# A third projection bank, mixed rows in pairs, and new orders in the token stage of an AdaLN-attention-FFN kernel

## The chip, the cores and the metric

One core of a Trainium2 chip runs the whole program. The metric is the device time of one execution in microseconds (us).

## The reference, cut to what matters

64 sequences of 64 tokens with 512 features pass through a conditioned mixing of tokens, a sparse attention and a residual, and then through a conditioned linear layer and a gated FFN with 4-bit weights and a second residual.

```python
h = einsum('bct,bcd->bdt', x, cond_weights[itok])          # tokens of a sequence mixed by a 64x64 matrix
q, k, v = h @ Wq + bq, h @ Wk + bk, h @ Wv + bv            # 16 query heads, 8 key heads of 32; rotary on q and k
mask = top 25 of 64 keys of each head by sigmoid(h @ Wr + br)
x1 = x + softmax(where(mask, q k^T / sqrt(32), -inf)) v @ Wo + bo
y = x1 @ W^T + scalings[i] * (x1 @ A[i]^T) @ Bm[i]^T       # i = adapter of the sequence
out = x1 + (gelu(y @ Wg^T) * (y @ Wu^T)) @ Wd^T            # 512 -> 4096 -> 512, weights dequantised on the chip
```

## The kernel before, in words

The program has a **token stage** and an **FFN stage**, one after the other on TensorE. The FFN stage (line 869, `product`, and line 886, `down_chunk`) is not touched by the change.

The token stage runs 16 iterations (`NT`) over tiles of 256 tokens, four sequences, which lie as two halves (q = 0, 1) of 128 rows. fp32 values are split into a high and a low part, and a product is three matmuls (high x high, high x low, low x high), so each value that comes out of PSUM and goes into a product passes twice: ScalarE copies the high part out (`mixed`, `heads_high`, `rows_high`), then VectorE subtracts it from the bank to get the low part (`mixed`, `heads_low`, `rows_low`) and frees the bank. Iteration t interleaves three tiles' work: the **body** of tile t (values v0, v1; scores; softmax; attention; output projection o0, o1), the **tail** of tile t-1 (adapter ranks xa and the linear layer h0 to h3, which go to DRAM in a combined form), and the **head** of tile t+1 (mixed rows hs0 to hs3, routing logits z, projections k0, k1, q0 to q3).

PSUM has eight banks, and all are used: two `proj` banks, which all the projections above take in the order of the list `USES` (20 uses, `BANK` gives the bank, `ready` waits until the previous use of the same bank was evacuated, `evacuated` waits for this use); two times two banks of `scores`, which the transposed probabilities share; one bank `pv` for probabilities times values; and one bank `turn` for x1 transposed.

The order is written out by hand on every engine, and the engines meet only at semaphores. On **TensorE**, `iteration` issues: `value` 0 and 1; `score` 0; `adapter_ranks`; `score` 1; `hidden_first` (h0, h1); `turn_probs` 0 (transposes of the softmax of half 0); `mixing` of chunks 0 and 1; `attend` 0; `mixing` of chunks 2 and 3; `routing`; k0, k1; `turn_probs` 1; `hidden_rest` (h2, h3); `out_proj` 0; `attend` 1; q0 to q3; `turn_rows` 0 (x1 of half 0 transposed); `out_proj` 1; `turn_rows` 1. `score` 0 waits for `q_ready`, that is for the low parts of q, one half of which VectorE makes in `q_low`.

On **VectorE**: values; `softmax_shift` 0 (row maximum, line 1248, and subtraction, line 1250); four steps of `dequantise` (lines 1156 to 1166); `mask_ranks`; `softmax_sum` 0 (line 1255); `ranks_low`; `normalise` 0 (line 1262), which releases `turn_probs` 0; `softmax_shift` 1; `mixed` of two chunks; three more steps of `dequantise` (lines 1169, 1172, 1176); `mixed` of the other two; `softmax_sum` and `normalise` 1; the last step of `dequantise`; `heads_low` 0; `rope` 0 (line 1213 on); `hidden_low` 0; `add_residual` 0; `top_keys`; `heads_low` 1; `rope` 1; `hidden_low` 1; `rows_low` 0; `add_residual` 1 (line 1278); `rope` 2; `q_low` (line 1223); `rows_low` 1. Iterations 0 and 1 dequantise a second unit of FFN weights.

On **ScalarE** among others: `exp`, `probs_turned` (line 987), `mixed` (line 947), `k_place` (eight copies on line 973, the last four of which wait for GpSimd's `k_low`, line 610), the copies of q0 to q3 out of PSUM with their bias (line 959), `rows_high`. On **GpSimd** each iteration begins when the store of x1 has landed (`x1_stored`): two adds of the residual (line 640), then the split or the combination of a unit of FFN weights (`store_unit`, lines 560 to 570), then the gathers of mixing matrices, `spread` (the combinations of h), `scale_unit`, loads, `k_low`, `spread`, `q_low`. `store_unit` is longest for a unit with odd k from 3 on (three combinations and three splits), which falls into iterations 2, 4, 8, 10 and 14. **SyncE** issues the transfers: logits out and in, h out, key bias out and in, x1 out.

## Time and profile before

| | before |
|---|---|
| median of 3 runs | 2682.28 us (2680.29 to 2684.94) |
| the profiled execution, its own time | 2682.33 us |
| its span in the trace | 2680.8 us |
| TensorE matmul busy | 2572.0 us (96%) |
| VectorE busy | 1963.3 us (73%) |
| ScalarE busy | 882.0 us (33%) |
| GpSimd busy | 977.0 us (36%) |
| token stage, to the first matmul of line 869 | 0 to 755.26 us |
| FFN stage | 755.26 to 2680.8 us |

The profile is one execution. [...] The share of busy time of a whole run says little here, since the two stages have different limits: the stretches of single iterations do. I cut the token stage at the starts of `score` 0 (line 731): 47.56, 93.24, 137.54, 182.87, 225.31, 271.25, 315.00, 357.48, 399.90, 445.19, 488.14, 534.03, 577.04, 619.98, 662.38 and 708.26 us for iterations 0 to 15.

### The profile page before, as it was taken

The numbers are of one execution on the slowest core, as the hardware profiler recorded it, in microseconds if no ns is written. First come the engines' busy times: TensorE is split into PE (matmuls) and PEld (weight loads), VectorE is DVE, ScalarE is ACT, GpSimd is POOL, SyncE is SP. The second block draws the span as 40 slices with busy tenths as digits, with TensorE's granted clock in tenths as the row PEclk, the third lists the DMA queues.
The fourth block names the chain that finished last, engine by engine and source line by source line (L and its number), as shares of the span: only waits on it lengthen the run. The fifth ranks groups of instructions, "written<-read, shape, count | busy, mean of one in ns | idle before, by whom it ended". The sixth has DMA issues, their size and how long they took to land.

```text
span 2680.8 us, 38725 instructions
## 1 busy us (share of the span) xinstructions
PE 2572.0 (96%) x13824; PEld 2163.0 (81%) x13824; DVE 1963.3 (73%) x3084; ACT 882.0 (33%) x1530; POOL 977.0 (36%) x1189
## 2 busy tenths in 40 slices
PE   5899999899889999999999999999999999999999
PEld 4788788788778888888888888888888888888887
DVE  6887878787768888888888888889754545454544
ACT  4445454444432222222222222222222222222222
POOL 3554435443445555545554555455500000000000
PEclk8999999999999999999999999999999999999999
DMA  3232222322598888786678667866557444565472
GB/s 121 77 102 93 91 97 91 105 78 92 188 335 315 331 322 327 275 336 236 242 276 330 242 239 279 324 243 238 208 191 276 186 156 150 220 244 194 175 260 102
DMA packets 167377, 562.27 MB, mean 210 GB/s; under 512 B 21784, under 2 KB 81048, under 8 KB 134560
## 3 DMA queue, kind: packets, MB, share of 16 engines
q1 hardware_dynamic: 131872, 458.10, 47.2%
q0 software_dynamic: 35328, 101.82, 10.2%
q8 instruction: 110, 1.80, 0.3%
q14 instruction: 67, 0.55, 0.1%
HBM read 427.27 MB, written 132.51 MB: 209 GB/s over the span
## 4 chain that ended last, share of the span: by engine, by line
PE 88%; DVE 8%; issue 2%; ACT 1%; SPq 0%; POOL 0%; DMA 0%; DVEq 0%; POOLq 0%; ACTq 0%
PE down L886 26%; PE bank_a L869 26%; PE bank_b L869 13%; PE proj L696 12%; PE bank_c L869 6%; PE scores L736 1%; PE pv L761 1%; PE scores L745 1%; DVE probs L1262 1%; DVE hs L1196 1%; DVE row_sum L1255 1%; DVE rope_sin L1216 1%; DVE row_max L1248 1%; ACT probsT L987 1%; DVE rope_in L1215 1%
## 5 line engine op out<-in xcount | busy, mean ns | idle before, releaser
L886 PE MATMUL down<-d_slot,inter_parts 128*128 128x512 f32 x3072 | 737.4, 389 | 0.0
L886 PEld LDWEIGHTS down<-d_slot,inter_parts 128*128 128x128 f32 x3072 | 576.6, 188 | 119.7
L1095 ACT ACTIVATE copy_p<-bank_a 128x512 f32<-128x512 f32 x384 | 229.7, 598 | 745.9 <-PE bank_a L869 745.9
L1404 DVE TENSOR_TENSOR acc<-down,acc 128x512 f32<-128x512 f32 x512 | 349.4, 686 | 67.4 <-PE down L886 60.1
L869 PE MATMUL bank_a<-h_ahead,gu_slot 128*128 128x512 f32 x1536 | 390.1, 389 | 2.5 <-ACT copy_p L1095 2.0
L869 PE MATMUL bank_a<-h_once,gu_slot 128*128 128x512 f32 x1536 | 390.0, 389 | 1.4 <-ACT copy_p L1095 1.4
L869 PEld LDWEIGHTS bank_a<-h_ahead,gu_slot 128*128 128x128 f32 x1536 | 288.1, 188 | 63.3 <-ACT copy_p L1095 2.9
L869 PEld LDWEIGHTS bank_a<-h_once,gu_slot 128*128 128x128 f32 x1536 | 288.1, 188 | 62.0 <-ACT copy_p L1095 2.2
L577 POOL TENSOR_TENSOR lut_v<-lut_v,signed_scale 128x512 f32<-128x512 f32 x96 | 123.9, 1290 | 422.1 <-DVE lut_v L1185 421.4
L1389 DVE TENSOR_TENSOR up<-gate,up 128x512 f32<-128x512 f32 x256 | 212.6, 830 | 88.9 <-ACT gate L1105 75.3
L1112 ACT ACTIVATE inter_parts<-up 128x512 fp32r<-128x512 f32 x256 | 160.3, 630 | 261.9 <-PE down L886 169.6
L1393 DVE TENSOR_TENSOR inter_parts<-up,inter_parts 128x512 fp32r<-128x512 f32 x256 | 186.9, 731 | 51.7 <-ACT inter_parts L1112 47.2
L562 POOL TENSOR_TENSOR w_parts<-lut_v,w_parts 128x512 fp32r<-128x512 f32 (+1 forms) x160 | 211.6, 1322 | 13.1
L1377 DVE TENSOR_TENSOR up<-bank_b,copy_p 128x512 f32<-128x512 f32 x128 | 87.8, 686 | 162.4 <-ACT copy_p L1095 141.0
L1105 ACT ACTIVATE gate<-bank_a 128x512 f32<-128x512 f32 x128 | 76.7, 599 | 374.5 <-PE bank_a L869 374.5
L869 PE MATMUL bank_b<-h_once,gu_slot 128*128 128x512 f32 x768 | 195.0, 389 | 0.0
L869 PE MATMUL bank_b<-h_ahead,gu_slot 128*128 128x512 f32 x768 | 194.9, 389 | 0.0
L869 PE MATMUL bank_c<-h_ahead,gu_slot 128*128 128x512 f32 x768 | 194.9, 389 | 0.0
L1370 DVE TENSOR_TENSOR gate<-bank_c,copy_p 128x512 f32<-128x512 f32 x128 | 88.5, 691 | 117.5 <-PE bank_c L869 114.3
L869 PEld LDWEIGHTS bank_b<-h_once,gu_slot 128*128 128x128 f32 x768 | 144.1, 188 | 30.3 <-DVE up L1377 0.4
L869 PEld LDWEIGHTS bank_c<-h_ahead,gu_slot 128*128 128x128 f32 x768 | 144.2, 188 | 30.0
L869 PEld LDWEIGHTS bank_b<-h_ahead,gu_slot 128*128 128x128 f32 x768 | 144.1, 188 | 30.0
(123 smaller groups left out, 3542.3 us busy)
## 6 DMA issues: line engine op xcount, KB each, us to landing
gu_slot<-w_scratch SPq DMA_DIRECT2D x128, 1792.0 KB, 7.6
d_slot<-d_scratch SPq DMA_DIRECT2D x64, 1024.0 KB, 9.8
w_scratch<-w_parts POOLq DMA_DIRECT2D x96, 512.0 KB, 4.3
h_ahead<-h_scratch SPq DMA_DIRECT2D x36, 1024.0 KB, 12.5
h_scratch<-h_out SPq DMA_DIRECT2D x32, 896.0 KB, 5.0
h_once<-h_scratch SPq DMA_DIRECT2D x27, 1024.0 KB, 7.9
acc<-out SPq DMA_DIRECT2D x18, 1024.0 KB, 5.5
out<-acc SPq DMA_DIRECT2D x18, 1024.0 KB, 11.6
```

What stands on the lines that cost most here:

```text
L562: pool.tensor_tensor(parts[:, :, LO, :], src, parts[:, :, HI, :].bitcast(F32), ALU.subtract).then_inc(w_step, 1)
L577: pool.tensor_tensor(lut_v[:, row], lut_v[:, row], signed_scale[:].bitcast(F32), ALU.mult).then_inc(w_step, 1)
L696: ins = pe.matmul(out_ap, lhsT, rhs, start=(start and n == 0), stop=(stop and n == len(pairs) - 1))
L869: ins = pe.matmul(bank[:], gu_slot[n % 2][:, w, u, c * P:(c + 1) * P], mat(v, h)[:, c, part, :], start=(start and c == 0 and i == 0), stop ...
L886: ins = pe.matmul(bank[:], inter_parts[:, j, u, q, e * P:(e + 1) * P], d_slot[m % 2][:, j, part, :], start=(j == 0 and i == 0), stop=(j == ...
L1095: act.activation(copy[:], bank_a[n % 2][:], ACT.Copy).then_inc(copied, 1)
L1112: act.activation(inter_parts[:, j, HI, q], up[:, q], ACT.Copy).then_inc(inter_hi[q], 1)
L1370: dve.tensor_tensor(gate[:, FIRST_HALF], bank_c[:], copy_p1[:], ALU.add).then_inc(gate_added[FIRST_HALF], 1)
L1377: dve.tensor_tensor(up[:, SECOND_HALF], bank_b[:], copy_p5[:], ALU.add).then_inc(up_added[SECOND_HALF], 1)
L1389: dve.tensor_tensor(up[:, q], gate[:, q], up[:, q], ALU.mult).then_inc(inter_done[q], 1)
L1393: dve.tensor_tensor(inter_parts[:, n % 2, LO, q], up[:, q], inter_parts[:, n % 2, HI, q].bitcast(F32), ALU.subtract) \
L1404: dve.tensor_tensor(acc[:, q, e], down[turn % 4][:], acc[:, q, e], ALU.add).then_inc(acc_added, 1)
```

## The change

The bank of `turn` is given up: `turn` becomes a view of the `pv` bank, and the free bank becomes a third `proj` bank. `attend` and `turn_rows` get a wait for each other's evacuation. The mixed rows come in pairs that fill a bank (`hs01`, `hs23`), so ScalarE and VectorE evacuate 512 columns at once, and `mixing` is issued whole ahead of `attend` 0. On TensorE `turn_rows` 1 moves from the end of its iteration to behind the two values of the next, h2 comes right behind `attend` 0 (h3 stays behind `turn_probs` 1). ScalarE and VectorE follow: `rows_high` 1 and `rows_low` 1 open the next iteration, h2's copy moves up, two of the four early steps of `dequantise` move behind the mixed rows, `mask_ranks` comes ahead of the other two, and VectorE's end of an iteration becomes `rope` 1, `rope` 2, `add_residual` 1, `q_low`, `rows_low` 0, `hidden_low` 1. SyncE stores x1 ahead of the second part of h.

```diff
@@ -151,12 +151,12 @@
             h_out = sb("h_out", [P, NM, 2, P], F32R)
-            proj = [ps(f"proj{i}", [P, 512], F32) for i in range(2)]
+            proj = [ps(f"proj{i}", [P, 512], F32) for i in range(3)]
 ...
             pv = ps("pv", [P, 2, 2, 2, C], F32)
-            turn = ps("turn", [P, KC, P], F32)
+            turn = pv[:].rearrange("p g r b c -> p g (r b c)").rearrange("p g (s n) -> p (g s) n", n=P)
@@ -191,8 +191,8 @@
         x_ld = [sem("x_ld0"), sem("x_ld1")]
-        proj_full = [sem("proj_full0"), sem("proj_full1")]
-        proj_free = [sem("proj_free0"), sem("proj_free1")]
+        proj_full = [sem(f"proj_full{i}") for i in range(3)]
+        proj_free = [sem(f"proj_free{i}") for i in range(3)]
@@ -236,10 +236,11 @@
         BODY = ["v0", "v1", "o0", "o1"]
-        HEAD = ["hs0", "hs1", "hs2", "hs3", "z", "k0", "k1", "q0", "q1", "q2", "q3"]
-        USES = ["v0", "v1", "xa", "h0", "h1", "hs0", "hs1", "hs2", "hs3", "z", "k0", "k1", "h2", "h3", "o0",
+        HEAD = ["hs01", "hs23", "z", "k0", "k1", "q0", "q1", "q2", "q3"]
+        USES = ["v0", "v1", "xa", "h0", "h1", "hs01", "hs23", "h2", "z", "k0", "k1", "h3", "o0",
                 "q0", "q1", "q2", "q3", "o1"]
-        BANK = {name: n % 2 for n, name in enumerate(USES)}
+        BANK = {name: n % 3 for n, name in enumerate(USES)}
+        PAIRS = {"hs01": (0, 1), "hs23": (2, 3)}
@@ -399,13 +400,13 @@
                     bias(t + 1)
-                if t > 0:
-                    store_hidden(t - 1, 1)
 ...
                 sp.dma_start(x1_v[t], x1[:]).then_inc(x1_stored, 16)
+                if t > 0:
+                    store_hidden(t - 1, 1)
@@ -696,21 +697,22 @@
-            def mixing(it, t, tt, par, chunks):
+            def mixing(it, t, tt, par):
 ...
                 pe.wait_ge(mix_ready, t * 2 + 2)
-                for c in chunks:
-                    bank, done = ready(it, f"hs{c}")
-                    for q in range(NP):
-                        ins = pe.matmul(bank[:, q * P:(q + 1) * P], x_in[:, par, q, c * P:(c + 1) * P],
-                                        mix_tile[:, par, q].rearrange("p b c -> p (b c)"), start=True, stop=True)
+                for name, pair in PAIRS.items():
+                    bank, done = ready(it, name)
+                    for n, c in enumerate(pair):
+                        for q in range(NP):
+                            ins = pe.matmul(bank[:, n * TOK + q * P:n * TOK + (q + 1) * P], x_in[:, par, q, c * P:(c + 1) * P],
+                                            mix_tile[:, par, q].rearrange("p b c -> p (b c)"), start=True, stop=True)
 ...
                 bank, done = ready(it, "z")
-                evacuated(pe, it, "hs2")
-                evacuated(pe, it, "hs3")
+                for name in PAIRS:
+                    evacuated(pe, it, name)
@@ -749,6 +751,7 @@
                 pe.wait_ge(pv_used, t * NP + q + PRIMED)
+                pe.wait_ge(turn_used, t * NP + PRIMED)
@@ -764,6 +767,7 @@
                 evacuated(pe, it, f"o{q}")
+                pe.wait_ge(pv_used, (t + 1) * NP + PRIMED)
@@ -795,10 +799,9 @@
-            def hidden_rest(it):
-                for n in (2, 3):
-                    hidden_main(it, n)
-                    hidden_adapter(n)
+            def hidden_rest(it, n):
+                hidden_main(it, n)
+                hidden_adapter(n)
@@ -807,6 +810,8 @@
                 value(it, 1)
+                if do_tail:
+                    turn_rows(t - 1, t - 1, 1)
@@ -819,16 +824,17 @@
                 if do_head:
-                    mixing(it, t + 1, tt_next, 1 - par, (0, 1))
+                    mixing(it, t + 1, tt_next, 1 - par)
                 attend(it, t, 0)
+                if do_tail:
+                    hidden_rest(it, 2)
                 if do_head:
-                    mixing(it, t + 1, tt_next, 1 - par, (2, 3))
 ...
                 if do_tail:
-                    hidden_rest(it)
+                    hidden_rest(it, 3)
@@ -838,9 +844,8 @@
                 out_proj(it, t, 1)
-                turn_rows(it, t, 1)
-
-            mixing(AHEAD, 0, 0, 0, range(KC))
+
+            mixing(AHEAD, 0, 0, 0)
@@ -855,9 +860,11 @@
             iteration(NT - 1, 1, 0, do_head=False)
+            turn_rows(NT - 1, NT - 1, 1)
 ...
             hidden_first(BEHIND, NT - 1)
-            hidden_rest(BEHIND)
+            hidden_rest(BEHIND, 2)
+            hidden_rest(BEHIND, 3)
@@ -941,10 +948,10 @@
-            def mixed(it, chunks):
-                for c in chunks:
-                    bank = full_wait(act, it, f"hs{c}")
-                    act.activation(hs[:, HI, c, :], bank[:, 0:TOK], ACT.Copy).then_inc(hs_hi, 1)
+            def mixed(it):
+                for name, (c, _) in PAIRS.items():
+                    bank = full_wait(act, it, name)
+                    act.activation(hs[:, HI, c:c + 2, :].rearrange("p k n -> p (k n)"), bank[:], ACT.Copy).then_inc(hs_hi, 1)
@@ -1016,6 +1023,8 @@
                 it = t
+                if do_tail:
+                    rows_high(t - 1, 1)
@@ -1025,11 +1034,11 @@
                 if do_head:
-                    mixed(it, (0, 1))
+                    mixed(it)
                 exp(t, 1)
-                if do_head:
-                    mixed(it, (2, 3))
                 heads_high(t, 0)
+                if do_tail:
+                    hidden(it, t - 1, 2)
@@ -1037,7 +1046,6 @@
                     hidden_high(t - 1, 0)
-                    hidden(it, t - 1, 2)
@@ -1054,7 +1062,6 @@
                     q_high(t + 1, 1)
-                rows_high(t, 1)
@@ -1062,7 +1069,7 @@
             split(3)
-            mixed(AHEAD, range(KC))
+            mixed(AHEAD)
@@ -1084,6 +1091,7 @@
             iteration(NT - 1, 1, do_head=False)
+            rows_high(NT - 1, 1)
@@ -1189,12 +1197,11 @@
-            def mixed(t, chunks):
-                for c in chunks:
-                    name = f"hs{c}"
-                    dve.wait_ge(hs_hi, t * KC + c + 1)
-                    dve.tensor_tensor(hs[:, LO, c, :], proj[BANK[name]][:, 0:TOK], hs[:, HI, c, :].bitcast(F32), ALU.subtract) \
-                       .then_inc(proj_free[BANK[name]], 1)
+            def mixed(t):
+                for name, (c, _) in PAIRS.items():
+                    dve.wait_ge(hs_hi, t * 2 + c // 2 + 1)
+                    hi, lo = (hs[:, u, c:c + 2, :].rearrange("p k n -> p (k n)") for u in (HI, LO))
+                    dve.tensor_tensor(lo, proj[BANK[name]][:], hi.bitcast(F32), ALU.subtract).then_inc(proj_free[BANK[name]], 1)
@@ -1295,22 +1302,22 @@
                 first, second = UNITS[t][0], (UNITS[t] + [None])[1]
+                if do_tail:
+                    rows_low(t - 1, 1)
 ...
                 softmax_shift(t, 0)
-                dequantise(*first, 0, 4)
 ...
                     mask_ranks(it, t - 1)
+                dequantise(*first, 0, 2)
 ...
                 if do_head:
-                    mixed(t + 1, (0, 1))
-                dequantise(*first, 4, DQ - 1)
-                if do_head:
-                    mixed(t + 1, (2, 3))
+                    mixed(t + 1)
+                dequantise(*first, 2, DQ - 1)
@@ -1329,14 +1336,13 @@
                     rope(it, t + 1, 1)
+                    rope(it, t + 1, 2)
+                add_residual(it, t, 1)
+                if do_head:
+                    q_low(t + 1)
+                rows_low(t, 0)
 ...
                     hidden_low(t - 1, 1)
-                rows_low(t, 0)
-                add_residual(it, t, 1)
-                if do_head:
-                    rope(it, t + 1, 2)
-                    q_low(t + 1)
-                rows_low(t, 1)
@@ -1345,7 +1351,7 @@
                               ALU.is_equal, ALU.mult).then_inc(const_made, 1)
-            mixed(0, range(KC))
+            mixed(0)
@@ -1359,6 +1365,7 @@
             iteration(NT - 1, do_head=False)
+            rows_low(NT - 1, 1)
```

## Rows read from the trace of the kernel before

**Rows 1.** Windows (us; busy and count of PE, PEld, DVE, ACT, POOL; PEclk; DMA): single stretches.
```profile
47.56:93.24 45.68, 35.51 (x265) 30.28 (x265) 37.95 (x69) 18.37 (x33) 11.98 (x14) 0.88 0.11 37
93.24:137.54 44.30, 40.75 (x337) 36.35 (x337) 40.26 (x74) 21.58 (x40) 22.80 (x27) 0.96 0.31 104
...
708.26:755.26 47.00, 38.21 (x284) 33.28 (x285) 22.58 (x33) 11.94 (x20) 13.35 (x21) 0.89 0.81 305
755.26:2680.80 1925.54, 1916.63 (x8448) 1585.12 (x8448) 1390.29 (x2034) 529.31 (x899) 653.28 (x790) 1.00 0.68 250
```
**Rows 2.** Windows of iterations 3, 5, 6, 7, 9, 11, 12, 13: one, and all eight's sum.
```profile
315.00:357.48 42.48, 39.20 (x336) 34.83 (x337) 33.37 (x65) 21.45 (x40) 17.20 (x21) 1.00 0.29 90
...
sum 342.39, PE 315.05 PEld 279.03 DVE 269.48 ACT 171.69 POOL 129.59; mean PE 39.38 PEld 34.88 DVE 33.69 ACT 21.46 POOL 16.20
```
**Rows 3.** Windows of iterations 2, 4, 8, 10, 14: one of them, and all five's sum.
```profile
225.31:271.25 45.94, 40.76 (x336) 35.90 (x337) 35.38 (x65) 21.44 (x40) 25.53 (x31) 0.96 0.30 100
...
sum 228.33, PE 204.17 PEld 179.38 DVE 175.75 ACT 106.69 POOL 121.05; mean PE 40.83 PEld 35.88 DVE 35.15 ACT 21.34 POOL 24.21
```
**Rows 4.** TensorE's waits in 0 to 760: waiter, releaser, us, times, longest.
```profile
PE proj L696 <- DVE hs L1196: 20.7, 16, 1.9
PE scores L731 <- DVE q_parts L1223: 16.8, 15, 5.7
PE turn L769 <- DVE x L1278: 13.6, 16, 1.8
...
PE scores L745 <- DVE probs L1262: 11.3, 12, 4.3
...
PE pv L761 <- ACT probsT L987: 5.6, 15, 1.2
```
**Rows 5.** Timeline of TensorE in iteration 6: start, us, line, tile, idle before.
```profile
324.42 1.09 PE L745 MATMUL scores<-identity,probs 128*128 128x128 f32 x8
...
330.28 1.53 PE L696 MATMUL proj<-hs,wr 128*16 128x256 f32 x12 [1.02 <-DVE hs L1196]
...
353.18 0.66 PE L769 MATMUL turn<-identity,x 128*128 128x128 f32 x4 [0.79 <-DVE x L1278]
```
**Rows 6.** The same in iteration 4: the routing matmuls.
```profile
242.50 2.63 PE L696 MATMUL proj<-hs,wr 128*16 128x256 f32 x12 [1.94 <-DVE hs L1196]
```
**Rows 7.** Critical chain: routing, k0 and k1 of iterations 4 and 6.
```profile
242.50 5.96 PE proj L696 x36
...
330.28 4.41 PE proj L696 x36
```
**Rows 8.** Timeline of VectorE in iteration 6: rope 1, hidden_low 1, q_low.
```profile
346.99 0.01 DVE L1213 LOAD_MASK_SELECT rope_sin<-rope_in  x1 [0.31 <-ACT rope_in L959]
...
350.59 1.09 DVE L1291 TENSOR_TENSOR h_out<-h_mats,h_out 128x896 fp32r<-128x896 f32 x1 [0.77 <-ACT h_out L1015]
...
356.53 0.69 DVE L1223 TENSOR_TENSOR q_parts<-rope_in,q_parts 128x512 fp32r<-128x512 f32 x1 [0.70 <-ACT q_parts L978]
```
**Rows 9.** Single lines over 50 to 756: ns min/median/max (dequantise, normalise).
```profile
L1164 DVE TENSOR_SCALAR signed_scale<-packed x18: 279/332/1380, 54.3 to 713.3; 128x256 int32<-128x256 int32 x18
L1262 DVE TENSOR_TENSOR probs<-probs,row_inv x32: 1210/1224/2298, 56.6 to 723.4; 128x1024 f32<-128x1024 f32 x32
```
**Rows 10.** Timeline of GpSimd: residual adds of iteration 4, k_low of iteration 8.
```profile
226.23 2.54 POOL L640 TENSOR_TENSOR x<-x_in,bo 128x512 f32<-128x512 f32 x2 [5.50 <-DMA out<-x]
426.91 1.40 POOL L610 TENSOR_TENSOR rope_in<-rope_in,k_whole 128x512 f32<-128x512 f32 x1 [1.40 <-ACT k_whole L963]
```
**Rows 11.** Timeline of ScalarE in iteration 6: k_place, second half.
```profile
342.01 2.55 ACT L973 ACTIVATE k_diagonal<-rope_in 32x512 fp32r<-32x512 f32 x4
```
**Rows 12.** Timeline of TensorE in iteration 15: turn_probs 1 and out_proj 1.
```profile
724.72 1.97 PE L745 MATMUL scores<-identity,probs 128*128 128x128 f32 x8 [2.85 <-DVE probs L1262]
...
737.79 2.97 PE L696 MATMUL proj<-wo,attnT 128*128 128x512 f32 x12 [0.94 <-DVE attnT L1266]
```
**Rows 13.** The same at the start: mixed rows of tile 0, second pair.
```profile
16.10 2.08 PE L706 MATMUL proj<-mix_tile,x_in 128*128 128x128 f32 x8 [1.59 <-DVE hs L1196]
```

## The prediction, made before the changed kernel was built or run

> **What bounds the kernel now.** The page comes first: TensorE is busy 96% of the span, but this is a mean over two stages. The windows separate them. In the FFN stage TensorE is busy 1916.63 of 1925.54 us at full clock [rows 1]; the change touches none of it, and there is nothing left to gain there. The token stage is different. Its inner iterations come in two kinds. Eight of them, which I call light (42.80 us on average, 342.39 / 8), hold 39.38 us of TensorE work [rows 2]. Five, which I call heavy (45.67 us, 228.33 / 5), have the longest work on GpSimd, 24.21 us against 16.20, and a granted clock of 0.96 instead of 1.00 [rows 2, 3]. In both kinds VectorE is busy only 34 to 35 us and ScalarE 21, so TensorE is the bound, together with the points at which it stands still.
>
> TensorE's waits name these points [rows 4], and the timeline of iteration 6 shows them in place [rows 5]. Of its 42.48 us it is idle 3.28 (42.48 - 39.20) [rows 2]. Four waits make 2.9 of that: 1.02 before the routing for the low parts of the mixed rows, 0.79 before `turn_rows` 1 for x1 [rows 5], 0.8 before `score` 0 for `q_low` (16.8 us in 15, of which one is 5.7) and 0.3 in `attend` 0 for the transposed probabilities (5.6 in 15, longest 1.2) [rows 4]. The rest, 0.4, lies inside `attend` and stays. So the floor of an inner iteration without the four is 42.5 - 2.9 = 39.6 us. The light mean lies 0.3 above iteration 6 because `turn_probs` 0 sometimes waits for `normalise` 0: 11.3 us in 12 waits, of which 4.3 in iteration 0 and 2.85 in iteration 15 [rows 4, 12].
>
> A heavy iteration costs 2.87 more than a light one. The routing waits 1.94 instead of 1.02 [rows 5, 6], and the 36 matmuls behind this wait take 5.96 us instead of 4.41, at the lower of the two clocks for a part of it [rows 7]: 0.92 + 1.55. The remaining 0.4 is a longer wait at `turn_probs` 0.
>
> **The change part by part.**
>
> *Mixed rows whole and ahead of `attend` 0, h2 behind it.* No matmul is added or dropped. Between the last mixing matmul and the routing now lie `attend` 0 (1.4 us) and h2 (15 matmuls, at 4.41 / 36 = 0.12 us each 1.8 us) [rows 7]: 3.2 us of cover for one ScalarE copy and one VectorE subtraction of 512 columns, about 0.6 us each by the like ones. Since `attend` 0 starts one pair of mixing matmuls later (0.9 us), the 0.3 wait for the transposed probabilities goes as well. The wait of 1.02, and in heavy iterations that of 1.94, goes; next due there is h2's evacuation before k1 reuses its bank, some 2 us early. With it the slow clock behind this wait goes, 1.55 in a heavy iteration: the wait of 1.94 is followed by it, that of 1.02 is not [rows 5 to 7]. What h2 covers is taken from behind `turn_probs` 1, where TensorE has other work.
>
> *`turn_rows` 1 behind the two values.* Its wait of 0.79 is covered by 24 value matmuls, 2.9 us. But VectorE now runs `rope` 2 ahead of `add_residual` 1, and `turn_rows` 1 must also find `rows_low` 0 done, which stands behind `q_low`; `score` 0 is queued behind it on TensorE, and with it everything. I count from `turn_probs` 0 (324.42 = T) [rows 5]. TensorE: `turn_rows` 1 started at T+28.76; without its wait (0.79) and the two above it (1.02, 0.3), plus 2.9 for the values, it is wanted at T+29.6. VectorE: `rope` 1 started at T+22.57 [rows 8]. It hangs on the copy of q1, which hangs on q1's matmuls (1.3 earlier) and on the end of `k_place` (T+20.14, now 0.3 earlier) [rows 11]; I take T+21.4. `q_low` started at T+32.11 [rows 8]. It loses the 1.1 of the earlier start, the 1.8 of `hidden_low` 1 and its wait, `rows_low` 0 with the small wait behind it (0.8), and the 0.6 of `add_residual` 1, which now hides in the wait for `q_high`: T+27.8. One subtraction for `q_low` and one for `rows_low` 0 end at T+29.1. Cover left over: 0.5 us. If it isn't enough, the excess is paid one for one.
>
> *`q_low` earlier.* `score` 0 wants it at T+30.0, it is there at T+28.4: the wait of 0.8 goes. Moved behind it are `hidden_low` 1, `rows_low` 1 and the values' additions; they end some 2.3 us after `score` 0 begins, just when the first softmax can begin, so they cost nothing as long as `turn_rows` 1 is on time.
>
> *Two `dequantise` steps fewer ahead of `softmax_sum` 0, two more behind the mixed rows.* A step takes 0.28 us alone and up to 1.38 [rows 9]. Ahead of `normalise` 0 this is worth 0.6 to 2 us, which is what the waits at `turn_probs` 0 are made of; but `softmax_sum` 0 can't start before `exp`. Behind the mixed rows the steps lie ahead of `normalise` 1, where none of the 13 inner iterations shows a wait [rows 4]. I take 0.1 to 0.2 us left over in light iterations. `normalise` takes 1.21 us, or 2.30 when disturbed [rows 9], and that is the 0.9 that I leave in the heavy ones.
>
> The stretched rows point to GpSimd: they stand beside its long work. [...]
>
> *SyncE and GpSimd.* x1 is stored ahead of h's second part, so nothing is queued in front of it. But `add_residual` 1 now comes relatively later: it ended 4.35 us before the next `score` 0 and will end 2.4 before. GpSimd starts its iteration 5.5 us behind it [rows 10], hence 2.0 later against `score` 0. In light iterations there is slack. In heavy ones GpSimd's `k_low` had 1.40 us to spare in iteration 8 [rows 10], the head's chain gets 2.5 faster (0.92 + 1.55) and GpSimd 2.0 later, so `k_low` comes 3.1 late, of which about 1.1 hides behind the first half of `k_place` (2.55 against `k_low`'s 1.40) [rows 10, 11]. The 2.0 left over shift the copies of q and the tail of VectorE, less the cover of 0.5 and what the wait at `turn_probs` 0 gives back: I take 0.9 per heavy iteration, between 0 and 2.5.
>
> *Third bank.* In the new order q2 reuses o0's bank and q3 that of q0; with two banks q1 waited for o0 and q2 for q0, and TensorE, now earlier against ScalarE, would have waited there. It gains nothing alone. *Shared bank.* `attend` waits for `rows_low` 1, done ten us before; `turn_rows` 0 waits for `heads_low` 1, which `out_proj` 1 needs 0.4 us later anyway. Price 0, but in iteration 15, where no q projection lies between, about 0.4 of the wait of 0.94 [rows 12] is paid twice.
>
> **The sum**, against the profiled execution (2682.33 us; 1.5 around its span of 2680.8):
> - light: floor 39.6 + 0.2 = 39.8, saved 3.0 x 8 = 24.0 (bounds 39.5 to 40.6: 26.4 to 17.6)
> - heavy: 39.6 + 0.9 + 0.9, rounded up to 41.5, saved 4.16 x 5 = 20.8 (40.3 to 43.0: 26.8 to 13.3)
> - iterations 0 and 1: VectorE is busy 37.95 and 40.26 us [rows 1] and sets the pace; ahead of `score` 0 it drops 0.7 and 1.8 us of work, and iteration 0 fills the routing wait: 3.7 (1.5 to 6)
> - iteration 15: h2 fills 1.8 of the 2.85 wait, of which VectorE's two extra steps take 0.4 back; less 0.4 for the shared bank, plus 2.0 of the slow clock behind that wait (8 transposes 1.97 instead of 1.09 and the matmuls after them) [rows 5, 12]: 3.0 (0.5 to 5.5)
> - before iteration 0: the wait of 1.59 between the two mixed pairs goes [rows 13]; weights are still loading and being split, so I take 1.0 (0 to 1.6)
>
> Together 52.5 us, bounds 33 to 66. The profiled execution is at the median of the runs (2682.33 against 2682.28), so no correction is needed: 2682.3 - 52.5 = 2629.8 us.
>
> **The rivals.**
> - *GpSimd becomes the limit of heavy iterations.* For it: a spare of only 1.40, 2.0 lost. Against: the first half of `k_place`. They stay at 44.0: 5 x 2.5 = 12.5 us less gain, 2642.
> - *VectorE meets GpSimd in new places.* The adds and splits of GpSimd now stand beside `softmax_sum` and `normalise` 0 instead of the steps before them. If each iteration pays one stretched `normalise` (1.09) and part of a stretched step, 1.4 in all for 13 iterations, the time is 2630 + 18 = 2648.
> - *The tail binds, and the clock falls with it (slower).* The place is `turn_rows` 1 behind the values, with `score` 0 behind it. If VectorE's chain to `rows_low` 0 ends 2.9 later than I count (0.5 cover), TensorE waits 2.4 at one point, and as behind the waits of 1.94 the slow clock adds 1.55: 3.95 against 2.9 saved, 13 x 1.05 = 14 slower, 2696. It decides from 1.9 late on (a wait of 1.4 with slow clock gives back the 2.9). Against it: I find no 1.9 us in this chain, whose steps are all in the trace.
> - *The waits only move* and the time stays at 2682: TensorE's order is strict, so a wait removed at one place may be met at the next. Against it: the covers worked out above.
>
> **How the numbers follow.** Forecast 0.64, GpSimd's limit 0.12, the new meetings 0.16, no change 0.03, slower 0.05. Of these the first three are faster: 0.92. A measurement of this kernel can tell 0.2%, 5.4 us, from no change. The range takes the bounds of the sum, 2616 to 2649, and both milder rivals: 2615 to 2650.
>
> **What would show it.** TensorE's waits for line 1196's rows and for `q_parts` and x gone from inner iterations; light iterations 39.6 to 40.0 us between `score` 0; PEclk 1.00 in iterations 2, 4, 8, 10, 14; the FFN stage at 1925.5 us. A wait of `turn_rows` 1 or of `score` 0 behind it above 0.5 us would prove the tail's count wrong; a wait of k_diagonal's second half for `k_low` above 2 us the first rival; a `normalise` of 2.3 us in light iterations the second.

## The result, and the profile after

The changed kernel takes 2646.5 us (median of 4 runs, 2645.14 to 2652.3) where the kernel before took 2683.61 in the same comparison (4 runs). The ratio is 0.987 [0.9858, 0.9882]: 1.3% faster. The profiled execution has a span of 2646.0 us against 2680.8, so 34.8 us went. The forecast was 52.5 us and 2629.8; the time lies inside the range of 2615 to 2650, at its upper edge. So the direction was right and a third of the gain is missing, and the question is where it stayed.

As before, I cut the token stage at the starts of `score` 0 (now line 733). In the rows PE is TensorE (PEld its weight loads), DVE VectorE, ACT ScalarE, POOL GpSimd and SP SyncE; "xN" counts instructions; brackets give the idle time of an engine before a row and who ended it; PEclk is the granted TensorE clock as a share of the full one. First single windows of the changed kernel (us; busy and count of PE, PEld, DVE, ACT, POOL; PEclk; DMA): iterations 0, 1 and 15 and the FFN stage, which answer to [rows 1].

```profile
44.75:92.50 47.75, 38.47 (x265) 32.47 (x265) 38.09 (x66) 17.14 (x28) 11.98 (x14) 0.80 0.10 33
92.50:136.78 44.28, 39.26 (x337) 34.93 (x337) 40.76 (x70) 21.42 (x37) 22.17 (x27) 1.00 0.26 84
675.47:720.24 44.77, 36.50 (x285) 31.86 (x285) 23.18 (x34) 12.46 (x21) 13.59 (x21) 0.92 0.85 319
720.24:2646.00 1925.76, 1916.96 (x8448) 1585.53 (x8448) 1391.69 (x2034) 529.61 (x899) 654.05 (x790) 1.00 0.67 250
```

Then the light iterations, which answer to [rows 2]: 3, 6 and 12 of the eight, and the sum.

```profile
178.45:220.56 42.11, 40.18 (x337) 36.31 (x337) 34.62 (x63) 21.07 (x37) 16.86 (x21) 0.96 0.30 95
...
304.15:344.86 40.71, 38.78 (x337) 34.86 (x337) 34.95 (x63) 21.07 (x37) 17.12 (x21) 1.00 0.31 94
...
551.78:593.88 42.10, 40.18 (x338) 36.17 (x337) 34.13 (x63) 21.07 (x37) 14.79 (x19) 0.96 0.29 90
...
sum 329.92, PE 314.54 PEld 283.21 DVE 278.00 ACT 168.58 POOL 130.13; mean PE 39.32 PEld 35.40 DVE 34.75 ACT 21.07 POOL 16.27
```

And the heavy ones, which answer to [rows 3]: 4 and 8 of the five, and the sum.

```profile
220.56:263.42 42.86, 40.62 (x337) 36.34 (x337) 36.12 (x63) 20.96 (x37) 25.07 (x31) 0.96 0.32 108
385.60:427.29 41.69, 39.07 (x338) 34.92 (x337) 37.12 (x63) 21.07 (x37) 24.33 (x30) 1.00 0.34 111
...
sum 208.77, PE 196.62 PEld 176.00 DVE 183.91 ACT 105.25 POOL 120.06; mean PE 39.32 PEld 35.20 DVE 36.78 ACT 21.05 POOL 24.01
```

Set beside the terms of the sum, the windows give this:

| term | predicted | measured |
|---|---|---|
| 8 light iterations | 24.0 | 342.39 - 329.92 = 12.5 |
| 5 heavy iterations | 20.8 | 228.33 - 208.77 = 19.6 |
| iterations 0 and 1 | 3.7 | 89.98 - 92.03 = -2.05 |
| iteration 15 | 3.0 | 47.00 - 44.77 = 2.2 |
| before iteration 0 | 1.0 | 47.56 - 44.75 = 2.8 |
| FFN stage | 0 | 1925.54 - 1925.76 = -0.2 |
| sum | 52.5 | 34.8 |

So the light iterations miss 11.5 us and iterations 0 and 1 miss 5.7; the rest is right within 2 us. TensorE's waits of the token stage (waiter, releaser, us, times, longest) say what is new, if laid beside [rows 4]:

```profile
PE pv L773 <- DVE x1T L1279: 28.5, 16, 2.7
...
PE proj L697 <- ACT rope_in L966: 6.0, 4, 4.2
...
PE scores L733 <- DVE q_parts L1230: 5.2, 1, 5.2
...
PE scores L747 <- DVE probs L1269: 2.8, 2, 2.6
PE proj L697 <- DVE wq L1198: 1.9, 1, 1.9
PE proj L697 <- DVE hs L1204: 1.5, 1, 1.5
...
PE pv L764 <- ACT probsT L994: 1.2, 1, 1.2
```

Three of the forecast's four waits are gone from the inner iterations: the routing's for the mixed rows (20.7 us in 16, now 1.5 in 1), `score` 0's for `q_low` (16.8 in 15, now only the first, 5.2) and `attend` 0's for the transposed probabilities (5.6 in 15, now 1.2 in 1). Most of `turn_probs`' went too (11.3 in 12, now 2.8 in 2). In their place `turn_rows` (line 773) waits 28.5 us in 16 for VectorE's low part of the rows, where it had waited 13.6 us for x. This is the first item of the forecast's own list of what would prove it wrong ("a wait of `turn_rows` 1 or of `score` 0 behind it above 0.5 us would prove the tail's count wrong").

The timeline of the end of iteration 6 (start, us, line, tile, idle before and releaser) shows the chain behind that wait. VectorE:

```profile
335.01 0.01 DVE L1220 LOAD_MASK_SELECT rope_sin<-rope_in  x1 [0.29 <-ACT rope_in L966]
...
337.15 0.69 DVE L1225 TENSOR_TENSOR rope_in<-rope_in,rope_sin 128x512 f32<-128x512 f32 x1
338.21 0.01 DVE L1220 LOAD_MASK_SELECT rope_sin<-rope_in  x1 [0.38 <-DVE rope_in L1225]
...
339.03 0.69 DVE L1222 TENSOR_TENSOR rope_in<-rope_in,cos 128x512 f32<-128x512 f32 x1
339.63 1.80 DVE L1223 TENSOR_TENSOR rope_sin<-rope_sin,sin 128x512 f32<-128x512 f32 x1
341.47 0.69 DVE L1225 TENSOR_TENSOR rope_in<-rope_in,rope_sin 128x512 f32<-128x512 f32 x1
342.08 0.68 DVE L1285 TENSOR_TENSOR x<-proj,x 128x512 f32<-128x512 f32 x1
342.86 0.69 DVE L1230 TENSOR_TENSOR q_parts<-rope_in,q_parts 128x512 fp32r<-128x512 f32 x1
343.47 0.68 DVE L1279 TENSOR_TENSOR x1T<-pv,x1T 128x512 fp32r<-128x512 f32 x1
```

GpSimd and TensorE in the same stretch:

```profile
339.11 1.78 POOL L616 TENSOR_TENSOR q_parts<-rope_in,q_parts 128x512 fp32r<-128x512 f32 x1 [7.74 <-ACT q_parts L985]
...
344.30 0.63 PE L773 MATMUL pv<-identity,x 128*128 128x128 f32 x4 [1.57 <-DVE x1T L1279]
```

With T = 313.44, where `turn_probs` 0 starts, `rope` 1 begins at T+21.57; the forecast said T+21.4. But `rows_low` 0 ends at T+30.71 and not T+29.1. Two things lie between that the count did not have. `rope` 2 stands directly behind `rope` 1 and begins 0.38 us after its last sum. Inside a rope, where an operation also waits for the one ahead of it, the gap is 0.03 to 0.04 us, so the dependence alone is not the price; between two ropes the program has three waits and three semaphore increments on VectorE's queue, and no run shows which of them takes the time. And the product with the sine takes 1.80 us instead of 0.68, beside GpSimd's own `q_low`, which itself takes 1.78. Against a cover of 0.5 us, 0.38 + 1.1 was too much. TensorE, too, was ready earlier, at T+29.29 and not T+29.6; `turn_rows` 1 starts at T+30.86, which is the wait of 1.57.

In the kernel before the same GpSimd operation ran beside other work. First VectorE, then GpSimd:

```profile
351.60 0.68 DVE L1272 TENSOR_TENSOR x1T<-turn,x1T 128x512 fp32r<-128x512 f32 x1
352.44 0.69 DVE L1278 TENSOR_TENSOR x<-proj,x 128x512 f32<-128x512 f32 x1 [0.15 <-PE proj L696]
...
351.64 1.29 POOL L615 TENSOR_TENSOR q_parts<-rope_in,q_parts 128x512 fp32r<-128x512 f32 x1 [9.53 <-ACT q_parts L978]
```

There VectorE read one operand from PSUM (`turn`, `proj`) and one from SBUF, and all three took their ordinary time (0.68, 0.69 and GpSimd's 1.29 us). The products of `rope` read both operands from SBUF. So the traces show a difference by the kind of operand: 1.80 us with two SBUF inputs, 0.68 and 0.69 with one. They also give the size of the stretch. Wherever a product or sum of a rope is stretched (in the changed kernel 22 times from 60 us on), it ends 0.54 to 0.56 us after the end of the GpSimd operation that was running when it began: 341.43 against 339.11 + 1.78 = 340.89 here. These products and sums began 0.03 to 0.62 us into GpSimd's operation, so what sets their end is the end of GpSimd's operation and not how long ago it began.

In heavy iterations GpSimd's `q_low` falls onto the product with the cosine instead, which then takes 1.53 or 1.54 us (1.82 in iteration 14) and not 0.69.

### The profile page after: what moved, and what is told of

The parts are those of the page before. It is cut to its first block, busy times and chain, and to the rows that moved or that the text cites. A ratio compares the mean times of both kernels' runs of the same rounds, so it can differ in the third digit from the quotient of the medians.

```text
span 2646.0 us, 38647 instructions
## 1 busy us (share of the span) xinstructions
PE 2562.0 (97%) x13824; PEld 2162.5 (82%) x13824; DVE 1982.4 (75%) x3052; ACT 876.3 (33%) x1498; POOL 977.0 (37%) x1189
## 4 chain that ended last, share of the span: by engine, by line
PE 84%; DVE 8%; ACT 4%; issue 2%; DMA 1%; POOL 0%; DVEq 0%; SPq 0%; ACTq 0%; POOLq 0%
PE down L893 26%; PE bank_a L876 26%; PE bank_b L876 13%; PE proj L697 7%; PE bank_c L876 6%; ACT k_diagonal L980 2%; PE scores L738 2%; DVE rope_sin L1223 2%; DVE rope_in L1222 2%; DVE rope_sin L1220 1%; DVE rope_in L1225 1%; PE proj L708 1%; PE pv L764 1%; DMA h_scratch<-h_out 1%; ACT rope_in L966 1%
## 6 DMA issues: line engine op xcount, KB each, us to landing
h_ahead<-h_scratch SPq DMA_DIRECT2D x36, 1024.0 KB, 12.5
```

## The experiments

The theory after the result: *VectorE's chain from `rope` 1 to `rows_low` 0 sets the end of an inner iteration, and GpSimd's `q_low` stretches it.* The rivals: that TensorE's own order (the clock, the banks) or VectorE's new order is what costs, and that the other moved steps brought less than I took. Times below are medians of 4 runs (experiment 6: 10; the last two: 5). The kernel before took 2683.92 us beside the first four kernels, 2683.55 beside the next three and 2683.45 beside the last two, so all ratios have the same base; a difference from the changed kernel is one from 2646.5.

**1. A narrow `q_low` on GpSimd.** It makes the low part for one of its four sequences only and leaves it out for the other three.

```diff
-            def q_low(t):
+            def q_low(t, blocks=NB):
...
+                pool.tensor_tensor(q_parts[:, LO, 0].rearrange("p b r c -> p r b c")[:, :, 0:blocks],
...
-                    q_low(t + 1)
+                    q_low(t + 1, 1)
```

> The changed kernel, in which GpSimd's q_low of the iterations computes one of the four sequences' columns only (the low part of half of q is left out for the other three). Theory: in the changed kernel TensorE's wait of 1.57 us at turn_rows 1 comes from VectorE's second rope behind the first, where the product with sin takes 1.80 us instead of 0.69 because it meets GpSimd's q_low (1.77 us). Then the product takes 0.7 to 0.9 us, the wait falls to about 0.5 us, and the time by about 1.1 us in 13 iterations, 12 to 18 us, to 2628 to 2635 (ratio to before 0.980 to 0.982). Rival: the wait is the length of the chain alone (ropes one behind the other, subtractions); then the product stays at 1.8 or something else takes its place, and the time stays at 2646 (0.987).

Measured: 2629.89 us, ratio 0.9803 [0.9785, 0.9821], 16.6 us less. VectorE and GpSimd, timeline near the end of an iteration:

```profile
328.20 0.01 DVE L1222 LOAD_MASK_SELECT rope_sin<-rope_in  x1 [0.38 <-DVE rope_in L1227]
...
329.62 0.96 DVE L1225 TENSOR_TENSOR rope_sin<-rope_sin,sin 128x512 f32<-128x512 f32 x1
...
329.10 0.93 POOL L616 TENSOR_TENSOR q_parts<-rope_in,q_parts 128x128 fp32r<-128x128 f32 x1 [7.74 <-ACT q_parts L987]
```

The product falls from 1.80 to 0.96 and `turn_rows`' waits from 28.5 to 13.4 us in 16. The collision is the cause of the larger part: 15.1 us of waits; the span is 19.0 us shorter (2627.0), the slow clock is gone from iterations 3, 4, 11 and 12, and a light iteration takes 39.9 us, where the forecast said 39.8. That the kernel lands on the forecast of 2629.8 is partly luck, since the 0.38 is still in it.

**2. `rows_low` 0 between the two ropes.** It moves work that TensorE needs first ahead, fills the 0.38 and shifts `rope` 2 against GpSimd. The three come together: this run does not part them.

```diff
                     rope(it, t + 1, 1)
+                rows_low(t, 0)
+                if do_head:
                     rope(it, t + 1, 2)
                 add_residual(it, t, 1)
                 if do_head:
                     q_low(t + 1)
-                rows_low(t, 0)
```

> The changed kernel with rows_low 0 between the two ropes on VectorE instead of behind q_low. Theory: turn_rows 1 then needs only add_residual 1 behind the second rope, the subtraction falls into the wait of 0.38 us between the ropes, and part of GpSimd's q_low passes meanwhile: score 0 starts 0.9 us earlier, 13 times, 2646 - 12 = 2634 us (ratio 0.982 to 0.984), and its wait is for q_parts. Rival: ScalarE's rows_high is so late that the second rope slips as far as is gained: 2644 to 2648 (0.986 to 0.988).

Measured: 2631.25 us, 0.9805 [0.9786, 0.9823], 15.3 us less with all work done. VectorE in the iteration that begins at 297.07:

```profile
331.36 0.69 DVE L1279 TENSOR_TENSOR x1T<-pv,x1T 128x512 fp32r<-128x512 f32 x1 [0.69 <-ACT x1T L1002]
...
332.75 1.03 DVE L1222 TENSOR_TENSOR rope_in<-rope_in,cos 128x512 f32<-128x512 f32 x1
333.71 0.68 DVE L1223 TENSOR_TENSOR rope_sin<-rope_sin,sin 128x512 f32<-128x512 f32 x1
```

A light iteration is 39.7 us long (297.07 to 336.76), just under the forecast's 39.8. GpSimd's operation (331.93 to 333.24) still meets `rope` 2, but costs 0.34 and not 1.1: 0.8 of its 1.31 us now runs beside the end of `rows_low` 0, which reads PSUM, and beside the shuffle. The new row to read is the first: VectorE now stands 0.69 us for ScalarE's copy.

**3. VectorE's old end of the iteration,** with the rest of the change kept.

```diff
                     rope(it, t + 1, 1)
-                    rope(it, t + 1, 2)
-                add_residual(it, t, 1)
-                if do_head:
-                    q_low(t + 1)
-                rows_low(t, 0)
                 if do_tail:
                     hidden_low(t - 1, 1)
+                rows_low(t, 0)
+                add_residual(it, t, 1)
+                if do_head:
+                    rope(it, t + 1, 2)
+                    q_low(t + 1)
```

> The changed kernel with VectorE's old end of an iteration (rope 1, hidden_low 1, rows_low 0, add_residual 1, rope 2, q_low), all else changed. The prediction's step: the new end brings q_low 2.6 us forward, so undoing it costs over 1.5 us in each of 13 iterations, 2665 us or more (ratio 0.993). Rival, by the trace of the changed kernel: the second rope meets GpSimd only in the new order and waits 0.38 us behind the first, so the new end gains nothing, 2643 to 2650 us (0.985 to 0.988).

Measured: 2644.76 us, 0.9855 [0.9836, 0.9873]. That can't be told from the changed kernel. TensorE's waits:

```profile
PE scores L733 <- DVE q_parts L1230: 33.9, 16, 6.2
```

The changed kernel waits 28.5 + 5.2 = 33.7 us for VectorE at `turn_rows` and `score` 0 together, this one 33.9 at `score` 0 alone. The new tail bought nothing as it stands: it moved the wait from one consumer to the other. (The new tail with `rows_low` 0 moved, experiment 2, is 13.5 us faster than the old one.) My step "*`q_low` earlier*: the wait of 0.8 goes" counted as a gain what was a change of place.

**4. Two projection banks** in the new order.

```diff
-            proj = [ps(f"proj{i}", [P, 512], F32) for i in range(3)]
+            proj = [ps(f"proj{i}", [P, 512], F32) for i in range(2)]
...
-        BANK = {name: n % 3 for n, name in enumerate(USES)}
+        BANK = {name: n % 2 for n, name in enumerate(USES)}
```

> The changed kernel with two projection banks instead of three, all else changed. The prediction's step: q2 and q3 then wait for the evacuation of q0 and q1 behind ScalarE's k_place, and the second value for add_residual 1, so the bank is needed for the new orders though it gains nothing alone. If TensorE's work is what bounds, two banks cost 0.8 us or more in 13 iterations, 2656 us or more (0.990). Rival: since VectorE's end of the iteration bounds, TensorE waits at another place but score 0 starts at about the same time: 2645 to 2651 us (0.986 to 0.988).

Measured: 2648.74 us, 0.987 [0.9852, 0.9888]: no difference from three banks.

```profile
PE proj L697 <- ACT rope_in L966: 18.3, 15, 3.7
PE proj L697 <- DVE x L1285: 17.1, 17, 4.1
...
PE pv L773 <- DVE x1T L1279: 2.6, 1, 2.6
```

The forecast was right that TensorE waits for banks then (35.4 us in two rows) and wrong that it matters: `turn_rows`' wait falls from 28.5 to 2.6. TensorE arrives later at a point where it would have waited anyway. As long as VectorE's chain ends the iteration, the third bank is worth nothing; whether it is in the order of 2 or 8, where this chain is shorter, no run shows.

**5. `turn_rows` 1 back at the end of its iteration,** ahead of the values.

```diff
                 value(it, 1)
-                if do_tail:
-                    turn_rows(t - 1, t - 1, 1)
...
                 out_proj(it, t, 1)
+                turn_rows(it, t, 1)
```

> The changed kernel with turn_rows 1 back ahead of the two values on TensorE. Theory: turn_rows 1 waits for rows_low 0, which VectorE reaches 1.57 us behind the point at which TensorE has finished the values; without the values as cover the wait becomes 1.57 + 2.9 = 4.5 us in 13 iterations: score 0 starts 2.9 us later each, 2646 + 38 = 2684 us or more with slow clock behind the longer wait (ratio 1.000 to 1.008). Rival: the head of the next tile does not hang on score 0 and takes the delay up: under 2665 us (0.993).

Measured: 2707.15 us, 1.0091 [1.0074, 1.0108], 60.6 us more than the changed kernel, and slower than the kernel before.

```profile
PE pv L773 <- DVE x1T L1277: 68.0, 15, 5.2
```

The row counts to 740 us; with the last one behind it, it is 69.5 us in 16, so the waits grow by 41.0 us for this line, and the mean granted clock falls to 0.981 (0.991 in the changed kernel): PEclk is 0.96 or 0.93 in all 13 inner iterations, where it was below 1.00 in four. The two values are 2.9 us of cover; without them VectorE's new order costs more than everything else brings, so the new order on VectorE needs this step. The reverse does not hold: with the old order on VectorE the step stands well (experiment 3, 2644.76 us). What the step is worth beside the old order no run shows.

**6. The mixing split again,** with `attend` 0 between the pairs and h2 back behind `turn_probs` 1. The list `USES` and ScalarE's order follow (left out here).

```diff
                 if do_head:
-                    mixing(it, t + 1, tt_next, 1 - par)
+                    mixing(it, t + 1, tt_next, 1 - par, ("hs01",))
                 attend(it, t, 0)
-                if do_tail:
-                    hidden_rest(it, 2)
                 if do_head:
+                    mixing(it, t + 1, tt_next, 1 - par, ("hs23",))
                     routing(it)
...
                 if do_tail:
+                    hidden_rest(it, 2)
                     hidden_rest(it, 3)
```

> The changed kernel with the mixed rows (still in pairs) one pair ahead of attend 0 and one behind it, and h2 back behind turn_probs 1 with h3; ScalarE follows. The prediction's step: the wait before the routing (1.0 us) comes back, and the slow clock behind it in the heavy iterations; since k0, k1 and rope 0 hang on the routing, it goes through to score 0: 1.0 to 1.3 us in 13 iterations plus up to 1.5 in 5, 2659 to 2671 us (0.991 to 0.995). Rival: the bound is VectorE's end of the iteration, so the wait is absorbed: 2646 to 2652 us (up to 0.988).

Measured: 2676.93 us, 0.9978 [0.9968, 0.9988] (10 runs), 30.4 us more than the changed kernel.

```profile
PE proj L697 <- DVE hs L1207: 24.7, 16, 2.1
PE pv L774 <- DVE x1T L1282: 18.1, 16, 2.4
...
PE pv L765 <- ACT probsT L996: 5.6, 15, 1.2
```

The two waits that the forecast removed here are back at their old size (20.7 and 5.6 in [rows 4]), the first even larger (a pair takes ScalarE 0.60 us and VectorE 0.69 to evacuate, one chunk in the kernel before took 0.38 and 0.42, which I take to be why). The span grew by 25.4 us (2671.4 against 2646.0). 23.2 + 4.4 of that are waits that come, 5.4 come at `turn_probs` (8.2 against 2.8), and 10.4 go at `turn_rows`: 22.6, with 2.8 left that these rows don't place. The two steps, pairs behind each other and h2, were undone together, so their shares stay open.

**7. The four early steps of `dequantise` back** ahead of `mask_ranks`.

```diff
+                dequantise(*first, 0, 4)
...
-                dequantise(*first, 0, 2)
...
-                dequantise(*first, 2, DQ - 1)
+                dequantise(*first, 4, DQ - 1)
```

> The changed kernel with four steps of dequantise and then mask_ranks ahead of softmax_sum 0, as before the change. The prediction's step: waits at turn_probs 0 come back, 0.3 us in light and 0.8 us in heavy iterations, 6 to 7 us in all, 2652 to 2654 us (0.988 to 0.989). Rival: GpSimd starts its iteration later than before the change, so the steps meet it more: 2.0 us per iteration, 2672 us (0.996).

Measured: 2654.11 us, 0.9892 [0.9874, 0.991], 7.6 us more. The intervals of the two ratios overlap by little ([0.9858, 0.9882] for the changed kernel), so the sign is likely and the size is not firm. The number is the expected one, the places are not. `turn_probs` waits 3.6 us in 7 instead of 2.8 in 2, only 0.8 more. In the profile (span 2650.6, 4.6 longer) the light iterations add 3.6 us and the heavy ones, for which I had expected 0.8 each, nothing (208.62 against 208.77).

**8. The high part of the rows first.** As 2, and ScalarE makes the high part of the rows ahead of that of the hidden.

```diff
-                if do_tail:
-                    hidden_high(t - 1, 1)
                 rows_high(t, 0)
                 if do_head:
                     q_high(t + 1, 0)
+                if do_tail:
+                    hidden_high(t - 1, 1)
+                if do_head:
                     q_high(t + 1, 1)
```

> The changed kernel with VectorE's rows_low 0 between the two ropes, and in addition ScalarE's high part of the rows (t, 0) ahead of its high part of the hidden (t-1, 1) at the end of an iteration. With rows_low 0 moved, VectorE stood 0.69 us waiting for ScalarE's x1T in front of rows_low 0 (seen at 331.36 us), because ScalarE still worked on the hidden's high part. Theory (the chain of VectorE from rope 1 to q_low sets the end of the iteration): the 0.69 goes; what TensorE still waits there is 0.55 us per iteration, so 0.3 to 0.55 us in each of 13 iterations, 4 to 7 us less than with rows_low 0 moved alone: 2624 to 2628 us. Rival (VectorE meets GpSimd): rope 2's products fall 0.7 us earlier, onto GpSimd's own q_low, and are stretched by 0.4 to 1.0 us as in the changed kernel: no gain or a loss, 2630 to 2634 us.

Measured: 2624.76 us (5 runs, 2622.8 to 2625.56), 0.9784 [0.9771, 0.9798]. This beats both kernels with all work done: 21.7 us less than the changed kernel. Two windows, a light and a heavy iteration, and then VectorE:

```profile
334.69:373.86 39.17, 38.56 (x336) 34.86 (x337) 33.37 (x63) 21.26 (x38) 16.21 (x20) 1.00 0.30 98
373.86:415.01 41.15, 39.51 (x336) 35.01 (x337) 37.16 (x63) 21.36 (x38) 24.46 (x30) 1.00 0.34 112
```

```profile
368.21 0.69 DVE L1280 TENSOR_TENSOR x1T<-pv,x1T 128x512 fp32r<-128x512 f32 x1
...
369.62 1.27 DVE L1223 TENSOR_TENSOR rope_in<-rope_in,cos 128x512 f32<-128x512 f32 x1
```

The 0.69 is gone, and the iteration shrinks by 0.5 us although the rival's collision is there as well: the cosine product takes 1.27 instead of 1.03. Both the theory and the rival were true, and the gain was the larger one. At 39.17 us, with a wait of 0.26 still in it, a light iteration lies below the 39.6 that I had called the floor.

**9. `dequantise` ahead of the mixed rows in iteration 0.** As 8, and in iteration 0 alone. In the changed kernel VectorE stood idle there with steps queued behind:

```profile
59.43 0.69 DVE L1204 TENSOR_TENSOR hs<-proj,hs 128x512 fp32r<-128x512 f32 x1 [2.01 <-ACT hs L954]
61.13 0.69 DVE L1204 TENSOR_TENSOR hs<-proj,hs 128x512 fp32r<-128x512 f32 x1 [1.02 <-ACT hs L954]
```

```diff
+                if not do_tail:
+                    dequantise(*first, 2, DQ - 1)
                 if do_head:
                     mixed(t + 1)
-                dequantise(*first, 2, DQ - 1)
+                if do_tail:
+                    dequantise(*first, 2, DQ - 1)
```

> As the kernel with the high part of the rows first, and in iteration 0 alone the dequantise steps 2 to 6 stand ahead of the mixed rows on VectorE. In the changed kernel VectorE stood idle 2.01 and 1.02 us in front of the mixed rows of iteration 0 (59.43 and 61.13 us), with these steps queued behind. Theory (VectorE sets the pace of iteration 0, and this idle time is why iteration 0 became longer by 2.07 us instead of shorter): the score of iteration 1 starts 1.5 to 2.5 us earlier, and the kernel takes 1.5 to 2.5 us less than with the high part first alone. Rival (the slow clock of iteration 0's mixing makes its length, not VectorE's queue): under 0.5 us of difference.

Measured: 2623.96 us (5 runs, 2623.06 to 2625.75), 0.9783 [0.9769, 0.9796]: no difference from 8. The forecast of 1.5 us or more is missed. But the trace does not speak against the idle time as a cause, since another thing changed between the two profiled executions: the clock during the 16 mixing matmuls of iteration 0 (1.95 us at the full clock, as at 314.37 in the changed kernel). In 8 the idle time was therefore 1.94 us and not the 3.03 of the changed kernel. Read from the timelines (us, to the start of `rope` 1 and from there to `score` 0 of iteration 1):

| kernel | mixing | start to `rope` 1 | `rope` 1 to end | iteration 0 |
|---|---|---|---|---|
| before | 1.92 + 1.16 | 36.63 | 9.05 | 45.68 |
| changed | 3.62 | 38.36 | 9.39 | 47.75 |
| experiment 2 | 3.62 | 38.34 | 8.36 | 46.70 |
| experiment 8 | 2.54 | 37.27 | 8.34 | 45.61 |
| experiment 9 | 3.62 | 36.80 | 8.35 | 45.15 |

At the same 3.62 us of mixing (experiments 2 and 9), `rope` 1 comes 1.54 us earlier with `dequantise` moved: the theory's 1.5 for this iteration. With the same order up to there (2 and 8), 1.08 us less mixing brings it 1.07 earlier: the rival is true as well. The cure of the tail shows from `rope` 1 to the end: 1.0 us in all three. What was gained in iteration 0 is not seen in the time, since iteration 1 then ran at PEclk 0.96 for 44.63 us, against 1.00 and 43.12 in 8. With one profile for each kernel, whether that clock hangs on the new order or on chance stays open.

## Why the prediction was right, and where it was off

- *The bound and the points where TensorE stands.* Right. The FFN stage moved by 0.2 us, and the gain is the removed waits.
- *Mixed rows whole, h2 behind `attend` 0.* Right: the waits of 1.02, 1.94 and 0.3 went in all inner iterations. With the slow clock of the heavy ones they make 29.5 us in the sum (8 x 1.32 + 5 x 3.79), and undoing the step costs 30.4 (experiment 6). That the two are so near is in part luck: 10.4 us of the returned waits were taken from `turn_rows`'.
- *`turn_rows` 1 behind the two values.* This is the step that failed. `rope` 1 came at T+21.57 (counted 21.4), but from there to `rows_low` 0 I counted 7.7 us, and it took 9.1. The count took durations from [rows 8], where the operations were separated by other work and ran beside nothing. In the new order 0.38 is the gap between two ropes back to back, and 1.1 is the collision. Experiments 1 and 2 settle it: either cure brings 15 to 17 us and light iterations of 39.7 to 39.9 us (forecast 39.8), which is the 11.5 of the light and part of the 5.7 of the first iterations.
- *The slow clock.* In light iterations 3, 11 and 12 and heavy 4 the wait was followed by it (PEclk 0.96, about 1.4 us each); in the other nine it was not, at waits as long (2.39 us even, ahead of iteration 2): 1.69 us stand ahead of iteration 3, which was slowed, and 1.69 ahead of iteration 9, which was not. I had the place in the third rival but with a wait of 2.4. Light iterations: 40.72 - 1.57 = 39.15 of floor, + 1.57 + 3 x 1.4 / 8 = 41.24, the measured mean.
- *The sizes of the floor.* 39.6 + 0.2 was too high: 39.15 measured, and in experiment 8 a whole iteration of 39.17 with a wait of 0.26 in it, so 38.9. The idle time inside `attend` is what I said (two rows of 0.18), but TensorE's busy time fell as well, from 39.20 [rows 2] to 38.78 and to 38.56 in experiment 8, for the same matmuls; which of the removed waits shortens their rows is not shown (experiment 3 has 38.56 too, with one long wait left). This error had the other sign and hid a part of the tail's: had the floor been 39.6, 13 x 0.45 us more would have made 2652 (an estimate), outside the range. That the time lies inside is luck to this extent.
- *Heavy iterations.* 41.75 on average where I said 41.5, but for other reasons. GpSimd's `k_low` is not late: ScalarE's second half of `k_place` follows the first without a pause (413.55 us, behind 411.01 + 2.53). The first rival is out. Instead VectorE meets GpSimd a second time in iterations 2, 8 and 10: the last sum of the key's rope takes 1.68 us in the chain of iteration 8, and everything to q3 shifts. (Iteration 4 has the slow clock instead, and 14, at 40.87 us, is as short as a light one: the five are not one kind any more.)

```profile
407.60 0.88 DVE rope_sin L1223
408.50 1.68 DVE rope_in L1225
...
417.27 1.70 PE L697 MATMUL proj<-hs,wq 128*128 128x256 f32 x12 [0.57 <-ACT rope_in L966]
```

  (The first two rows are from the critical chain, the last is from TensorE's timeline.) In experiment 8 the heavy iteration is still 1.98 us longer than the light one. 0.56 of it is this wait; the rest is not settled, and no run took the collision out of the key's rope.
- *The second rival's mechanism was right, its place wrong.* I put the new meetings at `softmax_sum` and `normalise` 0, 1.4 us an iteration, 2648. They came at the ropes, 1.1 + 0.38, and the time was 2646.5. What I missed is that an operation of mine can move onto GpSimd's, not only GpSimd's onto mine: I followed GpSimd's start and not `rope` 2's.
- *`q_low` earlier and the third bank.* No gain (experiments 3 and 4), and for the bank the forecast said "nothing alone". *The `dequantise` steps*: 7.6 us by experiment 7, near what I took, but in light iterations alone and hardly as waits of `turn_probs`: the mechanism is not confirmed. *Iterations 0 and 1*: 3.7 gained was the forecast, 2.05 lost the result. Of the 2.07 lost in iteration 0, 1.73 are lost ahead of `rope` 1 (38.36 against 36.63): VectorE stands idle for the pairs for 3.03 us, where it was 1.36 for the four chunks, and the mixing takes 3.62 us, where it was 1.92 + 1.16. The sum had no term for that. The other 0.34 lie behind, where the same tail takes 1.0 (9.39 against 8.36 in experiment 2). Experiment 8 has 88.73 us for both, against 89.98 before: 1.25 gained of the 3.7. *Iteration 15 and the start*: right within 2 us, with opposite signs.

## What to carry to other kernels

When a step is moved, lay its new neighbours on every engine beside it and ask what both read: here products and sums of a rope on VectorE, with both inputs in SBUF, were stretched by a GpSimd operation running at that time (0.94 to 1.82 us instead of 0.69), operations with an input in PSUM were not (128x512: 0.68 or 0.69 us), so put the latter beside GpSimd's work. Sort an engine's queue by who waits: one step that the bound engine needs first, moved ahead of one that it needs later, brought more here (21.7 us, with one such move on VectorE and one on ScalarE) than the third bank and the new tail as first built, which brought nothing that can be told. When a run removes an idle time and the total stays, compare the stretch itself, and at the same granted clock, before calling the cause wrong. And a wait that goes at one consumer is a gain only if the chain behind it gets shorter; else it stands at the next one, with the same sum.

## What the runs showed of the hardware

- A 128x512 fp32 product of two SBUF operands on VectorE takes 0.69 us alone and up to 1.82 beside a GpSimd operation of 1.29 with two SBUF operands. GpSimd's operation takes 1.77 to 1.79 in the eight light iterations, where it starts 0.1 us behind the start of such a product, and 1.29 to 1.31 where it does not. From 339.03 to 341.43 us VectorE does two products and GpSimd its one: 2.40, where 0.69 + 0.68 + 1.29 one after another make 2.66, so hardly anything ran in parallel.
- How much a collision costs depends on how much of GpSimd's operation is left. A stretched product ends 0.54 to 0.56 us after it, in the changed kernel and in experiments 1, 2, 3 and 8 alike: 1.80 when the product starts 0.5 us into GpSimd's operation, 0.96 when that operation has a quarter of the columns, 1.03 and 1.27 in the orders of experiments 2 and 8.
- Operations with an input in PSUM are not stretched: 142 of them overlap an arithmetic operation or a cast of GpSimd in the changed kernel's token stage, and the longest of a kind is within 0.02 us of its median (0.68 to 0.69 us for 128x512, 1.21 to 1.23 for the row maximum and its subtraction). Nor is a shuffle, with one SBUF input (0.72 to 0.76). An int32 operation with one SBUF input, 128x256 (line 1164), is: 0.28 us alone, 1.22 at 309.14, beside GpSimd's operation from 308.91 to 310.21.
- `rope` 2's first operation directly behind `rope` 1's last begins 0.38 us after it; one independent subtraction between them fills the gap (experiment 8: the subtraction from 368.21 us, 0.69 long, `rope` 2 from 368.83, and no idle time).
- TensorE stood still for 1.55 to 1.70 us ahead of iterations 3 to 14. The lower granted clock followed in 4 of these 12 and not in 8, nor behind the 2.39 us ahead of iterations 1 and 2. In experiment 8, where it stands for 0.2 to 0.4 there, iterations 3 to 14 are all at 1.00.
